# Local attention in a two-block adaLN network: every stage of its pipeline in another slot, the late normalisation and the residual's transposition among them

## What is computed

```python
for i in range(DEPTH):                                   # DEPTH = 6
    x = attn_layer(shift_tokens(x), Wqkv[i], q_scale[i], k_scale[i], Wo[i]) + x
    x = ffn_layer(shift_tokens(x), ln_g[i], ln_b[i], W1[i], b1[i], W2[i], b2[i]) + x

def attn_layer(x, Wqkv, qs, ksc, Wo):                    # 16 heads of 64
    q, k, v = split(x @ Wqkv)
    q = l2norm(q) * qs; k = l2norm(k) * ksc
    q = q * cos * scale + rotate_half(q) * sin * scale
    k = k * cos * inv + rotate_half(k) * sin * inv
    # windows of 32 tokens, each sees itself and the one before
    out = softmax(mask(q @ k.T * 8)) @ v
    return out @ Wo

def ffn_layer(x, ...):
    a, gate = split(layernorm(x) @ W1 + b1)              # 341 each
    return (a * gelu(gate)) @ W2 + b2
```

## Time and profile before

| | us |
|---|---|
| median of 3 runs | 4757.02 (4753.99 to 4761.74) |
| the profiled execution | 4742.66, its span 4740.9 |
| PE busy | 4207.0 (89%) |
| DVE busy | 4008.7 (85%) |
| ACT busy | 3751.7 (79%) |
| POOL busy | 3521.7 (74%) |

### The profile page before, as it was taken

One profiled execution on the slowest core, in us unless ns is written; L12 is line 12 of the kernel. 1 busy time (PEld: TensorE's weight loads), 2 busy tenths in 40 slices (PEclk: granted clock), 3 DMA queues, 4 the chain that ended last, 5 costly groups with the idle time before them and its releaser, 6 DMA issues. The chain is left out here.

```text
span 4740.9 us, 124337 instructions
## 1 busy us (share of the span) xinstructions
PE 4207.0 (89%) x45166; PEld 3132.2 (66%) x45166; DVE 4008.7 (85%) x7658; ACT 3751.7 (79%) x11543; POOL 3521.7 (74%) x2504
## 2 busy tenths in 40 slices
PE   6988699999999999999999999999899997688887
PEld 3555477777777777777777777777777775445453
DVE  4676798989988889889889899888998895598887
ACT  1555588888888888888888888888888886777774
POOL 0010699999999889988999999999899894444444
PEclk8999799999999999999999999999999998788888
DMA  1000111112111121111111111111111111000000
GB/s 26 7 6 2 47 51 39 45 40 57 52 40 45 43 54 50 42 44 45 52 46 45 43 47 51 47 45 40 50 51 41 45 39 31 0 4 3 3 3 5
DMA packets 118569, 168.67 MB, mean 36 GB/s; under 512 B 26563, under 2 KB 44422, under 8 KB 118022
## 3 DMA queue, kind: packets, MB, share of 16 engines
q1 hardware_dynamic: 109246, 160.92, 12.8%
q10 hardware_dynamic: 8776, 0.45, 0.1%
HBM read 20.79 MB, written 2.10 MB: 5 GB/s over the span
## 5 line engine op out<-in xcount | busy, mean ns | idle before, releaser
L1380 POOL TENSOR_TENSOR b_w<-b_w,b_vt 128x512 f32<-128x512 f32 x768 | 1190.5, 1561 | 273.7 <-DVE b_ss L1295 143.2
L1384 POOL TENSOR_TENSOR b_rn<-b_ssm,all_neg_half 128x16 f32<-128x16 f32 x384 | 1174.9, 3060 | 32.0
L1177 ACT ACTIVATE b_Pr<-ps,b_nm 128x96 f32<-128x96 f32 x3072 | 1002.6, 353 | 0.6
L1177 ACT ACTIVATION_READ_ACCUMULATOR b_Pr<-ps,b_nm 128x1 f32 x3072 | 676.0, 220 | 0.0
L1220 ACT ACTIVATE b_PT<-ps 96x512 f32<-96x512 f32 x768 | 456.8, 595 | 259.7 <-PE ps L1029 246.6
L992 PE MATMUL ps<-all_ident,b_w 128*128 128x128 f32 x3072 | 454.7, 278 | 175.4 <-DVE b_xtok L282 109.0
L1063 PE MATMUL ps<-b_Whi,b_xlo 128*128 128x512 f32 x1152 | 572.3, 497 | 34.5 <-DVE b_vt L1293 19.5
L1343 DVE TENSOR_TENSOR b_Pr<-b_Pr,b_rinv 128x384 f32<-128x384 f32 x768 | 541.7, 705 | 26.3
L1029 PE MATMUL ps<-all_ident,b_Pr 128*96 128x128 f32 x3072 | 475.7, 277 | 62.8 <-ACT b_PT L1220 45.2
L1291 DVE TENSOR_TENSOR b_w<-ps,until_b_rotab 128x512 f32<-128x512 f32 x768 | 523.5, 682 | 8.9 <-ACT b_sq L1197 4.8
L1293 DVE TENSOR_TENSOR b_vt<-ps,until_b_rotab 128x512 f32<-128x512 f32 x768 | 521.8, 679 | 0.0
(11 more groups left out here) (259 smaller groups left out, 9365.4 us busy)
## 6 DMA issues: line engine op xcount, KB each, us to landing
b_V<-b_Vraw SPq DMA_DIRECT2D x384, 192.0 KB, 2.6
b_V<-b_Vraw SPq DMA_DIRECT2D x384, 128.0 KB, 2.4
b_V<-b_Vraw SPq DMA_DIRECT2D x192, 64.0 KB, 2.2
b_Wraw<-in_L_ffn_Wqkv SPq DMA_DIRECT2D x36, 256.0 KB, 3.3
b_Wo<-in_L_ffn_Wo SPq DMA_DIRECT2D x6, 512.0 KB, 4.2
a_xtok<-in_L_attn_hidden_states SPq DMA_DIRECT2D x16, 128.0 KB, 2.1
out<-c_xout SPq DMA_DIRECT2D x16, 128.0 KB, 1.8
b_W<-in_L_ffn_W SPq DMA_DIRECT2D x6, 341.0 KB, 3.5
```

The costliest lines, as they stand in the source:

```text
L1177: last = nc.scalar.activation(s.Pr[:, r % 2, j, i], ps[:, S_BANK[j], i * KEYS:(i + 1) * KEYS], ACT.Exp, bias=s.nm[:, r, j, i:i + 1], accum ...
L1380: nc.gpsimd.tensor_tensor(rows, rows, s.vt[:, i % 4], ALU.add).then_inc(s.pool_add, 1)
L1384: nc.gpsimd.tensor_tensor(s.rn[:, j], s.ssm[:, j], g.neg_half[:, 0:HB], ALU.pow).then_inc(s.pool_r, 1)
```

## The change

Only the tables of slots are changed; no instruction is added, removed or given another shape.

```diff
-QK_SLOT = {0: (0, 0), 2: (0, 2), 6: (1, 0), 8: (1, 2), 16: (0, 1), 17: (0, 3), 22: (1, 1), 24: (1, 3)}
-V_SLOT = {15: (0, 4), 21: (1, 4), 29: (0, 5), 30: (1, 5)}
-ROTATE_LAG, ADD_LAG = 2, 2
+QK_SLOT = {0: (0, 0), 3: (0, 2), 6: (1, 0), 8: (1, 2), 15: (0, 1), 18: (0, 3), 22: (1, 1), 24: (1, 3)}
+V_SLOT = {14: (0, 4), 21: (1, 4), 28: (0, 5), 30: (1, 5)}
+ROTATE_LAG, ADD_LAG = 3, 0
...
-XT_SLOT, XN_SLOT, W2_SLOT = 21, 31, 29
-TRANSPOSE_SLOT = {22: (0, 0), 26: (1, 2), 27: (1, 0), 28: (0, 2)}
+XT_SLOT, XN_SLOT, W2_SLOT = 23, 30, 29
+TRANSPOSE_SLOT = {23: (0, 2), 24: (1, 0), 26: (1, 2), 27: (0, 0)}
...
-SCORE_LAG, EXP_LAG, SCALE_LAG, TURN_LAG, VALUE_LAG, COPY_LAG = 0, (4, 5), (7, 8), (8, 11), 14, 15
+SCORE_LAG, EXP_LAG, SCALE_LAG, TURN_LAG, VALUE_LAG, COPY_LAG = 0, (2, 5), (7, 8), (8, 11), 15, 16
...
-RES_SLOT, STATS_SLOT, END_SLOT, SPLIT_SLOT = 14, 24, 31, 8
-DVE_NORM_SLOT = {27: 2}
-DVE_LATE_NORM_SLOT = {4: 3}
-POOL_NORM_SLOT = {7: 0, 16: 1}
-GELU_SLOT, RSTD_SLOT, GATE_SLOT = 21, 23, 19
+RES_SLOT, STATS_SLOT, END_SLOT, SPLIT_SLOT = 12, 23, 30, 8
+DVE_NORM_SLOT = {29: 2}
+DVE_LATE_NORM_SLOT = {1: 3}
+POOL_NORM_SLOT = {6: 0, 16: 1}
+GELU_SLOT, RSTD_SLOT, GATE_SLOT = 21, 23, 20
```

More of the change, by code:

```diff
@@ L723 @@
 CONVERT_SLOT = {1: (2,), 4: (3,), 7: (4,), 10: (5,)}
-LATE_SLOT = {0: (0, 3), 4: (0, 1), 6: (1, 3), 7: (1, 1)}
-WO_SLOT = (11, 12)
-W1_SLOT = {5: 0, 17: 2, 21: 1}
-XT_SLOT, XN_SLOT, W2_SLOT = 21, 31, 29
-TRANSPOSE_SLOT = {22: (0, 0), 26: (1, 2), 27: (1, 0), 28: (0, 2)}
-READ_LAG = 0
-SCORE_LAG, EXP_LAG, SCALE_LAG, TURN_LAG, VALUE_LAG, COPY_LAG = 0, (4, 5), (7, 8), (8, 11), 14, 15
-RES_SLOT, STATS_SLOT, END_SLOT, SPLIT_SLOT = 14, 24, 31, 8
-DVE_NORM_SLOT = {27: 2}
-DVE_LATE_NORM_SLOT = {4: 3}
-POOL_NORM_SLOT = {7: 0, 16: 1}
-GELU_SLOT, RSTD_SLOT, GATE_SLOT = 21, 23, 19
+LATE_SLOT = {1: (0, 1), 3: (0, 3), 6: (1, 1), 7: (1, 3)}
+WO_SLOT = (10, 12)
+W1_SLOT = {4: 0, 20: 2, 21: 1}
+XT_SLOT, XN_SLOT, W2_SLOT = 23, 30, 29
+TRANSPOSE_SLOT = {23: (0, 2), 24: (1, 0), 26: (1, 2), 27: (0, 0)}
+READ_LAG = 0
+SCORE_LAG, EXP_LAG, SCALE_LAG, TURN_LAG, VALUE_LAG, COPY_LAG = 0, (2, 5), (7, 8), (8, 11), 15, 16
[4 more added lines that the diff above has]
+GELU_SLOT, RSTD_SLOT, GATE_SLOT = 21, 23, 20
 def piece_slots():
```

## The result

The changed kernel takes 4812.0 us (median of 4 runs, 4809.8 to 4812.61), the kernel before in the same job 4755.51 us (4750.54 to 4761.74): ratio 1.0118, 95% interval 1.0105 to 1.0132. It is slower, by 56.5 us; forecast were 4817 and +60. The profiled execution took 4809.8 us, its span 4808.0, 67 more than the profiled one before.

What follows compares the result with a forecast made beforehand. POOL was taken to bound each step; the late normalisation ahead of the rotations ties a 36.4 us ring against 35.77, so 96 x 0.63 = +60 us, 4817 us on the median's scale, range 4748 to 4885.

Steps and rivals of the forecast that it cites:

- The ring's length: Cycle n3 (POOL's fourth inverse norm of a sequence), DVE's late normalisation, two rotations, POOL's work to next n3: 36.4 us.
- The price taken for the second addition: POOL's second addition, no longer beside DVE's late normalisation, was taken to need 1.28 us in place of 2.19.
- Together 36.4 us, in short and long steps alike: Every step, with or without GELU, was to take 36.4 us against a mean of 35.77 before.
- +0.63 as a mean: Growth forecast for each of 96 steps, 36.4 against 35.77 us, giving +60 us in all.
- The wait for n3: Sign: DVE's late normalisation waits 1 to 2 us in each step for POOL's fourth inverse norm.
- I cost both at nothing: POOL's fifth addition earlier and layer norm's products behind the seventh: zero cost, PE having over 3 us to spare.
- PE's removed wait is worth nothing: Moving the residual's transposition removes PE's 1.17 us wait for L282; worth nothing in the sum.
- one wait of 2 to 2.5 us for the first rotation: PE's removed 1.2 us were to come back as this wait at slot 6.
- no cost, no gain: Values a slot later, first exponentials of each round two slots earlier, other slots: zero effect.
- POOL is what a step waits for: Kernel before: POOL works 22.82 or 22.62 us without a gap per step; the other engines stand beside it.
- Rival 1: Faster: POOL reaches n3 before DVE arrives, the ring opens, PE's removed wait saves 112 us: 4645 us; chance 0.17.
- The special case of rival 4: DVE's second scaling waits for the end of n0, POOL's first inverse norm: 310 us more, 5067; chance 0.01.

Runs made afterwards that it cites:

- Experiment 1: Kernel before with only the late normalisation moved to slot 1, ahead of both rotations: 4810.77 us, ratio 1.0137.
- experiment 2: Changed kernel with ACT's GELU replaced by a copy of the same shape: 4768.73 us, one execution.
- experiments 5: Changed kernel with late normalisation behind both rotations, its two turnings at slots 7 and 9, first exponentials back at lag 4: 4812.03 us, ratio 1.0136.
- experiment 6: Changed kernel, late normalisation behind both rotations, its turnings later, first exponentials at lag 4, layer norm's products again ahead of the seventh addition: 4763.38 us, ratio 1.0036.
- experiment 3: Kernel before with only the residual's transposition, its statistics and the turnings behind it in the changed order: 4748.59 us, ratio 1.0001.
- the first of 7: Kernel before with the late normalisation at slot 7, behind the first scaling, and its two turnings at slots 9 and 10: 4842.29 us, ratio 1.0203.
- experiment 8: Kernel before with the clamp of the sums of squares moved from POOL to DVE: 5057.97 us, ratio 1.0662.
- experiment 9: Both kernels with POOL's four powers replaced by products of the same shape: 5007.99 and 5021.9 us, one execution each.

## Why the prediction was right, and where not

Right in the result (4817 forecast, 4812.0 measured) and in the mechanism of the short steps, with two errors of size that cancelled.

- **The ring's length.** Forecast 13.7 + 22.7 = 36.4 us; the trace has 13.48 + 22.50 = 36.0. The price taken for the second addition, 1.28 us in place of 2.19, held. Experiment 1 shows that the late normalisation's move alone is enough for the loss.
- **"Together 36.4 us, in short and long steps alike, since the ring holds neither PE nor ACT"**: this step failed. The ring is the same in all steps, but a maximum is taken over rings, and long steps were already held by a longer one. They take 36.59 us; with the GELU replaced by a copy they take 36.0 like the others (experiment 2). The right sum has more terms: 40 short steps grew by 1.26 us each, +50; 36 long steps shrank by 0.21 each, -8, and a lower clock (last section) added 13; the borders added 5. So +0.63 as a mean came out near by luck: it was made of a short step forecast too long by 0.4 us and a long one too short by 0.2, before the clock.
- **The wait for n3, "1 to 2 us in each step"**: 0.33 us, in every second step. In experiment 1, without the other moves, it is 1.35.
- **"I cost both at nothing", on POOL's list**: this step failed, unseen in the total. The layer norm's product behind the seventh addition makes a second ring, 35.87 us in the short step, just under the first. I had excused it by PE's spare 3 us; but PE has those spare over a whole step, not at this point, where it takes its next work straight to DVE. While the first ring stands the second costs nothing, and only opening both brings the short step back to 34.77 (experiments 5 and 6). Opening only the second was not tried; nearest to it is experiment 1, where the layer norm stands in its old place and the first ring alone gives 36.29 us.
- **PE's removed wait is worth nothing**: right in the total (experiment 3), where a gain of some 13 us and a lower clock's 16 us cancel; the price of the clock was not in the sum, which had nothing won or lost by it. But it does not come back as one wait of 2 to 2.5 us for the first rotation. It comes as waits for ACT's stores in long steps and for L291 in short ones, and about 1 us a step for L1293 in several pieces.
- **Values and exponentials, "no cost, no gain"**: for the values about right in short steps, where experiment 6 keeps their move and has +1.3 us over 40 steps. The exponentials' move is not tested by it: experiments 5 and 6 both put the first group back to lag 4. In long steps the moves that are left, the transposition's among them, are not free (+3.2) and at the borders neither (+10.4). Which of them makes the borders longer wasn't taken apart.
- **"POOL is what a step waits for"** in the kernel before: not shown. The two experiments that took work or a meeting from POOL in that kernel (the first of 7, and 8) were expected to shorten the short step and lengthened it; both brought new meetings and waits, so they don't refute it either. What sets its 34.73 us stays open.
- **The rivals.** Rival 1 needed n3 ahead of DVE's score reduction. It needed 1.3 us; the reduction came 1.0 us later in the change, and so left only 0.33 of wait, but late for the same reason that cost the time. The special case of rival 4, the second scaling waiting for the end of n0, didn't happen: it asked for steps of 39 us, and away from the layer borders the longest is 37.62.

## What to carry to other kernels

In a software pipeline over several engines, write down the cycles through the dependences, one for each order on each engine, and take the longest for each kind of step; a wait on an engine outside the longest cycle can be removed or added for nothing, and a move that seems free may be a second cycle waiting just under the first. An experiment that opens one cycle and changes no time has not refuted it (here 36.00 us became 35.87, and 34.77 only with the second cycle open): look for the wait that is left in the trace, open that too, and only then judge. Before an operation is moved between two engines that hamper each other, look who starts first where they meet, and by how much. And where a moved wait makes PE idle in another place, look at its granted clock before the loss is put down to the wait.

## What the runs showed of the hardware

**Who starts first.** A lead of 0.16 us of DVE gives a stretched addition on POOL, a lead of 0.04 us of POOL a stretched normalisation on DVE; with the second meeting, and the lower clock that came with it, the kernel takes 5058 us in place of 4744 (experiment 8). The Trainium skill (SBUF: State Buffer, section on the two separate sides) describes the shared port pair as an exclusive lock held by whoever starts first for the whole instruction. For products and additions the traces agree: 1.28 becomes 2.19 us, 1.21 becomes 2.32, a statistics product of two columns 0.16 becomes 1.46. For POOL's power they don't: a scaling of DVE took 0.56 us wholly inside a power of 2.93. Here the measurement decides: this power let DVE through. That a kernel whose POOL is full of powers meets DVE less than one with short work is what experiment 9 suggests.

**The clock.** Of 36 long steps of the change, 13 take about 37.6 us in place of 36.59. The stretch table, one microsecond to a row, shows the beginning of such a step; columns as in the earlier trace rows.

```profile
2000.00:2001.00 1.00, 0.10 (x1) 0.10 (x2) 0.91 (x2) 1.00 (x3) 1.00 (x2) 1.00 0.75 219
2001.00:2002.00 1.00, 0.56 (x4) 0.32 (x4) 1.00 (x3) 1.00 (x3) 1.00 (x2) 1.00 0.06 16
2002.00:2003.00 1.00, 0.63 (x4) 0.64 (x5) 1.00 (x3) 1.00 (x3) 1.00 (x1) 0.78 0.00 0
2003.00:2004.00 1.00, 1.00 (x7) 0.94 (x6) 1.00 (x3) 0.98 (x2) 0.92 (x3) 0.50 0.00 0
2004.00:2005.00 1.00, 1.00 (x4) 0.81 (x4) 1.00 (x2) 0.99 (x4) 1.00 (x2) 0.50 0.00 0
2005.00:2006.00 1.00, 1.00 (x4) 0.81 (x3) 0.54 (x1) 1.00 (x8) 1.00 (x1) 0.51 0.00 0
2006.00:2007.00 1.00, 1.00 (x6) 0.87 (x6) 0.00 (x0) 1.00 (x3) 0.92 (x3) 1.00 0.00 0
```

The granted clock is 0.50, the lower level of 1.2 GHz, for about 3.4 us, and a projection product takes 0.63 us in place of 0.40. Ahead of it PE stood idle in two gaps, both behind ACT's stores (L1147), as the timeline of PE has them:

```profile
2000.90 0.66 PE L992 MATMUL ps<-all_ident,b_w 128*128 128x128 f32 x4 [1.08 <-ACT b_qkT L1147]
2002.37 0.97 PE L992 MATMUL ps<-all_ident,b_w 128*128 128x128 f32 x4 [0.81 <-ACT b_qkT L1147]
```

Of the 36 long steps the clock falls in none of the kernel before, in 13 of the change (13 us in all), in 20 with the transposition alone (16 us), in none with the late normalisation alone, and in none of the change with the GELU replaced by a copy. So the transposition's move, which puts PE's waits behind ACT's GELU and stores, brings the lower clock, and that is a price I had not in the sum. It is not the only move that does: in the first run of experiment 7 the clock falls without it too, in 12 long and 14 short steps, and in experiment 8 in all of them. In the step that begins at 2073.59 the gaps are nearly the same, 1.06 and 0.81 us, and the clock stays at 1.00; what tells the two apart stays open.
